# Pairing attention steps into one visit, with a third buffer of probabilities

## The reference

```
xn  = layernorm(x) * ln1_g + ln1_b
q, k, v = split(xn @ w_in.T + b_in)            # 16 heads of 16
scores  = q @ k.T / 4
allowed = (row % 8 == 0) | (row == column)
attn    = softmax(where(allowed, scores, -inf))
x1 = x + (attn @ v) @ w_out.T + b_out
h  = gelu((layernorm(x1) * ln2_g + ln2_b) @ w1.T + b1)  # 1024 wide
x2 = x1 + h @ w2.T + b2
x  = layernorm(x + x2)
y  = top-1 of 8 experts: relu(x @ wi.T + x @ lora_A[e].T @ lora_B[e].T) @ wo.T + wo_b
out = layernorm(x + y)
```

## Time and profile before

| what | value |
| --- | --- |
| median of three runs | 1440.81 us |
| span of the profiled execution (its own time, first to last instruction) | 1437.3 us |
| median less this span | 3.5 us |
| TensorE busy | 1386.3 us, 96% of the span |
| TensorE weight loads | 1066.3 us, 74% |
| VectorE, ScalarE, GpSimd busy | 854.4, 734.6, 647.8 us |
| granted TensorE clock, mean | 0.995 |
| attention stages, batches 0 to 3 | 150.1, 171.5, 171.5, 150.0 us |

### The profile page before, as it was taken

The page is one execution under the profiler, slowest core; times in us unless marked ns, Lnnn a source line. Parts: engine busy times, 40 slices in busy tenths (PEclk is TensorE's granted clock), DMA queues, the critical chain, the costliest instruction groups (busy, mean ns, idle before and its releaser), DMA issues.

```text
span 1437.3 us, 26412 instructions
## 1 busy us (share of the span) xinstructions
PE 1386.3 (96%) x10103; PEld 1066.3 (74%) x10103; DVE 854.4 (59%) x1823; ACT 734.6 (51%) x1103; POOL 647.8 (45%) x533
## 2 busy tenths in 40 slices
PE   6799999999999999999999999999999999999997
PEld 5688665678888766668888866667888876556996
DVE  6748576636656666555647576763675657762332
ACT  3444555553544555564444555555444455655442
POOL 3554321328754414145865432333776442132755
PEclk9899999999999999999999999999999999999999
DMA  7565223215561132212682213220556212310100
GB/s 246 161 181 107 57 45 67 55 38 192 190 164 47 50 68 51 56 45 84 210 214 62 74 38 75 57 53 20 189 189 158 74 45 44 80 26 23 52 16 30
DMA packets 91394, 130.51 MB, mean 91 GB/s; under 512 B 8314, under 2 KB 68180, under 8 KB 88148
## 3 DMA queue, kind: packets, MB, share of 16 engines
q1 hardware_dynamic: 91268, 128.82, 32.9%
HBM read 68.08 MB, written 60.57 MB: 90 GB/s over the span
## 4 chain that ended last, share of the span: by engine, by line
PE 79%; DVE 10%; POOL 4%; issue 2%; ACT 2%; DMA 0%; SPq 0%; POOLq 0%; DVEq 0%; ACTq 0%
PE ps L1567 19%; PE ps L1568 16%; PE ps L1569 16%; PE ps L1756 8%; PE ps L1745 7%; PE ps L1730 4%; DVE mx L1442 3%; PE ps L1803 2%; PE ps L1791 2%; PE ps L1825 2%; DVE stats L1316 2%; POOL rows L1042 1%; ACT prob L1172 1%; PE ps L1688 1%; PE ps L1762 1%
## 5 line engine op out<-in xcount | busy, mean ns | idle before, releaser
L1442 DVE TENSOR_REDUCE mx<-ps 128x2 f32<-128x1024 f32 x256 | 311.1, 1223 | 179.0 <-PE ps L1730 176.9
L1172 ACT ACTIVATE prob<-ps 128x1024 f32<-128x1024 f32 x256 | 262.6, 1026 | 180.4 <-PE ps L1745 180.2
L1057 POOL TENSOR_TENSOR hid1l<-gel,hid1h 128x512 fp32r<-128x512 f32 x85 | 111.2, 1309 | 202.2 <-ACT hid1h L1214 202.1
L1057 POOL TENSOR_TENSOR hid2l<-gel,hid2h 128x512 fp32r<-128x512 f32 x85 | 111.1, 1307 | 197.6 <-ACT hid2h L1214 197.5
L1057 POOL TENSOR_TENSOR hid0l<-gel,hid0h 128x512 fp32r<-128x512 f32 x86 | 112.4, 1307 | 191.6 <-ACT hid0h L1214 191.5
L1206 ACT ACTIVATE gel<-ps,cols 128x512 f32<-128x512 f32 x128 | 88.2, 689 | 180.7 <-PE ps L1569 169.5
L1745 PEld LDWEIGHTS ps<-qslot,kslot 50*128 50x128 f32 x1024 | 76.2, 184 | 91.0 <-issue 65.8
L1208 ACT ACTIVATE gel<-ps 128x512 f32<-128x512 f32 x128 | 76.6, 598 | 120.9 <-PE ps L1825 119.7
L1756 PE MATMUL ps<-prob,vals 128*32 128x256 f32 x2048 | 137.5, 385 | 0.2
L1745 PE MATMUL ps<-qslot,kslot 50*128 50x256 f32 x1024 | 128.9, 330 | 4.2 <-ACT prob L1172 4.1
L1730 PE MATMUL ps<-kslot,qslot 48*128 48x512 f32 x512 | 105.8, 424 | 4.8 <-DVE mx L1442 4.4
(11 more groups left out here) (245 smaller groups left out, 3943.9 us busy)
## 6 DMA issues: line engine op xcount, KB each, us to landing
k_d<-kst SPq DMA_DIRECT2D x192, 128.0 KB
kslot<-k_d SPq DMA_DIRECT2D x64, 384.0 KB
xin<-in_L_attn_x SPq DMA_DIRECT2D x32, 256.0 KB, 4.3
rows<-xs_d SPq DMA_DIRECT2D x16, 512.0 KB, 6.3
y_d<-rows SPq DMA_DIRECT2D x15, 512.0 KB, 3.1
rows<-y_d SPq DMA_DIRECT2D x15, 512.0 KB, 4.5
out<-rows SPq DMA_DIRECT2D x15, 512.0 KB, 3.2
xs_d<-xin SPq DMA_DIRECT2D x28, 256.0 KB, 2.7
```

The source lines that it names most:

```text
L1057: nc.gpsimd.tensor_tensor(hid[i % RING][1][:], gel[i % 2][:], hid[i % RING][0][:], ALU.subtract).then_inc(lo_done, 1)
L1172: nc.scalar.activation(prob[(n - 1) % 2][:].rearrange("p e i q -> p (e i q)"), ps[:, 0:2, :].rearrange("p a n -> p (a n)"), ACT.Exp).then_ ...
L1442: nc.vector.tensor_reduce(best[:, :, j % NQ], ps[:, at:at + 2, :], AX.X, ALU.max).then_inc(maxr_done, 1)
```

## The change

A new function `visit` takes the place of `step`. It does two steps at once: maxima and scores of step s, the weighted sums of steps s - 2 and s - 1, then scores and maxima of step s + 1. Step 1 has a visit of its own. Visits come at every second part of an item beside two blocks (parts 1 and 3), and at every third part beside three. A third buffer `prob2` lies over the two tiles `x1o`; the exponentials go round three buffers and wait for the weighted sums of three steps before. ScalarE waits, at step 2 of each batch, for the stores from `x1o`, and GpSimd waits, before the first x1 of the next batch is written, for the last weighted sums.

```diff
+PB = 3
...
-        def step(s):
-
-            if s % 2 == 0:
+        def visit(s):
+
+            maxima(s)
+            scores(s)
+            if s > 1:
                 weighted(s - 2)
                 weighted(s - 1)
-            scores(s)
-            maxima(s)
-            turns(s)
-            moves(s)
+                scores(s + 1)
+                maxima(s + 1)
+            for one in (s, s + 1)[:1 + (s > 1)]:
+                turns(one)
+                moves(one)
...
-            ahead = min(2, quarter // 2) if len(blocks) == 2 else 0
-            while s < STEPS_B and s * 4 * n <= (quarter + ahead) * STEPS_B:
-                step(s)
-                s += 1
+            ahead = 1 if len(blocks) == 2 else 0
+            if s < STEPS_B and s // 2 * 8 * n <= (quarter + ahead) * STEPS_B:
+                visit(s)
+                s += 1 + (s > 1)
...
+        prob.append(place("prob2", [P, 2, 2, QW], F32, r1 + 8192)[0])
...
+                    if b and PLACE[c] < 3:
+
+                        pool.wait_ge(av_done, N("at", b - 1, PAIRS - 1, KK - 1))
...
+                    elif a[1:] == (0, 2):
+
+                        for k in range(2):
+                            act.wait_ge(x1st[k], max(v for (bb, _), (j, v) in X1_STORE.items() if j == k and bb == b))
+                        act.wait_ge(xs_done, N("stx", b, CHUNKS[-1]))
                     else:
-                        act.wait_ge(av_done, n - 2)
-                    nc.scalar.activation(prob[(n - 1) % 2][:].rearrange("p e i q -> p (e i q)"),
+                        act.wait_ge(av_done, n - PB)
+                    nc.scalar.activation(prob[(a[1] * KK + a[2]) % PB][:].rearrange("p e i q -> p (e i q)"),
                                          ps[:, 0:2, :].rearrange("p a n -> p (a n)"), ACT.Exp).then_inc(exp_done, 1)
...
-                            last = mm(ps[at:at + PR, OUT, 0:QW], vals[:, v:v + PR], prob[(n - 1) % 2][:, e, i, :],
+                            last = mm(ps[at:at + PR, OUT, 0:QW], vals[:, v:v + PR], prob[(p * KK + kk) % PB][:, e, i, :],
                                       start=kk == 0, stop=kk == KK - 1)
```

## The result

The changed kernel takes 1489.32 us (median; runs from 1483.27 to 1492.47) where the kernel before took 1439.82 beside it: a ratio of 1.0338, interval 1.0316 to 1.036, slower by some 49 us. The forecast was 1471 in a range of 1438 to 1492. The profiled execution spans 1487.5 us, 50.2 more than before.

A forecast was written before the change was run, and what follows sets the result against it. TensorE was taken as the path in the attention stages. Eight terms summed to +30.4 us on the profiled 1437.3, giving 1467.7 of span; with 3.5 carried along for the median, 1471 us was forecast, range 1438 to 1492.

The forecast's parts named there:

- changes of tiling: On TensorE, a visit switches between full-array and packed matmuls less often, saving 0.20 us per visit: -24.8 us.
- wait for the exponential: A visit's second scores wait 0.19 us for the exponential of the first, 124 times: +23.6 us.
- VectorE: Second maxima need the first reduced; layer-norm and pick chains eat the 0.6 us margin in places: +3 us.
- third sign: The third stated condition for the forecast being wrong: VectorE's maxima become the longest wait.
- late behind that wait: Maxima and the next matmul follow scores that waited more slowly, 0.19 us more in 100 visits: +19 us.
- waits that go: In two-block batches, the 52 earlier waits of scores for the exponential end: -12.5 us.
- copies in the UP bank, two blocks: The next up matmul waits for ScalarE's copy of a single transpose, 0.46 us each, 28 times: +12.9 us.
- three-block transposes: Four transposition steps per three-block batch follow another in the UP bank with no visit between: +7 us.
- Rival B: TensorE's queue is refilled while scores wait, so the +19 us falls away: 1452 us, chance 0.20.
- Rival D: At a visit's second scores, the exponential is ready in time; 23.6 and 19 us fall away: 1428 us, chance 0.09.
- Rival C: The wait of scores also swallows the first pair's 0.10 us change of tiling, a further -12.4 us: 1440, chance 0.09.
- At nothing: The third buffer over x1's staging, with its ScalarE and GpSimd waits, and the loads and stores cost nothing.

The follow-up runs named there:

- all three edits: The changed kernel with halved reductions (half of the maxima's input left out), scores ahead of maxima, and the hidden copy behind a transposition's copy: 1429.99 us, ratio 0.9935.
- one moved step: The changed kernel with the hidden tile's copy put behind a transposition's copy on ScalarE at part 3: 1479.58 us, ratio 1.0272.

## Why the prediction came out as it did

The sign held, and so did the changes of tiling and the wait for the exponential inside a visit. The range held by 2.7 us at its upper end, and that was luck: the sum of 30.4 us met 50.2, and two of its terms were wrong in opposite directions. A term of +19 that was not there stood in for the lateness of VectorE, which was put at +3, and for the clock, which was in no term. That the two-block stage came out at 156.3 for 157 was luck of the same kind: its share of the +19 (25 times 0.19, some 5 us) was not there, and in batch 0 maxima waiting for VectorE (4.4 us) and the clock (at most 1.7) brought as much. By its own third sign (VectorE's maxima as the longest wait) the forecast was wrong.

| term | forecast, us | what the runs showed |
| --- | --- | --- |
| fewer changes of tiling | -24.8 | each interval of the visit as counted; 4.3 of 6.2 us found over a three-block stage (all three edits) |
| wait for the exponential | +23.6 | 0.19 in the visit; 19 us when 100 of 124 visits are spared it |
| "late behind that wait" | +19 | 0: maxima follow after 0.34 |
| waits that go | -12.5 | not seen alone; most of each was the wait of maxima for VectorE |
| copies in the UP bank, two blocks | +12.9 | 7.3 + 3.0 in the waits; 9.7 won by one moved step |
| first down half shortened | +2.2 | not tried alone |
| three-block transposes | +7 | `ot` 1.69 behind `tn` once and 0.81 behind `ga` twice per batch, 6.6 in both |
| VectorE | +3 (at most +12) | 22.8 less 4.4 in waits, and the clock behind them |

*What is late behind that wait* failed, and it failed in the reading. Two rows (the scores that waited, the maxima 0.43 later) were taken for cause and effect, and the reduction that ended 0.05 us ahead of the maxima was not looked at. Halved reductions, which leave the waits of the scores as they were, put the maxima back at 0.34. The second 0.43 of that row, from the maxima to the next matmul, goes with them: in the changed kernel it is 0.42 to 0.44 behind 23 of the 24 late maxima, and 0.32 to 0.35 behind 78 of the 80 others. So a wait does delay what follows, but the wait is that of the maxima. The rule of the Trainium skill that was weighed there ("TensorE: Matmul & The Clock Gate", on engine queue depths: weight loads are pulled ahead of matmuls in flight) was the better guide, and the trace agrees: behind scores that waited 0.89 the load came after 0.23 and the maxima after 0.34. Rival B was right on this step, though not in its time of 1452.

*VectorE* was the right mechanism and mis-sized. The margin of 0.6 us between first and second maxima was nearly right (0.43 in the visit above, where the reduction ends at 1227.20), but I asked how often a chain of 2 us meets a visit, and not where VectorE's other work goes when both reductions of a visit lie 2.1 us apart: all of it (negated maxima, sums' division, layer norm, picks, the low halves) falls into the one gap between visits, and what does not fit is paid by the second maxima. Before, it had a gap behind each reduction. That account is read from the timelines; what was tried is the reductions: halving them takes 29.7 us off the changed kernel and 16.3 off the kernel before.

*The clock* was in no term. The clock columns of 0.96 and 0.99 are shares of 1.00 and 0.50. In the trace the clock stands at 0.50 for 37.4 us of the four attention stages, 17.0 of them in batch 1, so that at most half of that, 19 us, was lost. With the waits gone, it goes too, but for one stretch of 3.4 us.

Rival D is out, since scores started 0.06 us behind an exponential that ended late. Rival C is out too: scores that waited still took 0.34 to the next start, the change of tiling included. *At nothing* held for the buffer.

What stays open: why the ways in and out of visits saved 4.3 us and not 6.2 over a three-block stage, and what makes a wait of 2 us bring the clock down.

## What to carry to other kernels

Two steps merged into one visit save changes of tiling (0.20 us per visit here, and no total shows it), but each of them also owned a gap in which ScalarE and VectorE caught up; count what every engine has to finish between the two uses of a bank, all of its queue included, and not only the one instruction waited for. A late start has a releaser: look for the instruction that ended 0.05 us ahead of it on any engine before you give it to the wait in front. Here the third buffer was worth more for moving the sums into the shorter of two gaps (8 us less) than for merging the gaps (49 us more).

## What the runs showed of the hardware

TensorE's granted clock fell to 1.2 GHz inside stages where TensorE was over 90% busy, mostly behind single waits of 1.5 us or more (2.08 us, then 6.7 us at 0.50), and not behind each of them (2.10 us, then 20 us at 1.00). In the kernel before, whose longest wait for maxima on TensorE's row was 0.8 us, the attention stages have none of it.

Scores that had waited 0.89 us on ScalarE delayed nothing behind them: maxima followed after 0.34, as behind scores that had not waited. Maxima that had waited on VectorE were followed after 0.43 instead of 0.32 or 0.33. Why the one and not the other was not tried.

Twice a tiny VectorE operation took seven times its usual time, behind the start of an addition on GpSimd. In the changed kernel, in batch 1, and then the same operation in batch 3:

```profile
499.68 1.27 POOL L1032 TENSOR_TENSOR x1g<-xg,crow 128x512 f32<-128x512 f32 x1
499.78 1.20 DVE L1470 TENSOR_TENSOR negs<-negm,negs 128x4 fp32r<-128x4 f32 x1
...
1239.19 0.17 DVE L1470 TENSOR_TENSOR negs<-negm,negs 128x4 fp32r<-128x4 f32 x1
```

It started 0.10 us behind GpSimd's addition and ended 0.03 us after it (500.98 and 500.95), and so it went again at 862.35 in batch 2. The same operation takes 0.16 or 0.17 with GpSimd at rest, and also where a GpSimd operation begins after it (three times); two more of them took 0.49 beside another GpSimd operation. That lengthens the very queue that maxima wait for; it was not tried by itself.
